# Causal masks of an attention kernel: added in VectorE's maximum instead of by mask products on TensorE

## The reference

```
o1 = _attn(q, k1, v1, causal)          # all keys up to the query's own
o2 = _attn(q, ks, vs)                  # 128 selected keys, no mask
winmask = causal & (ii[:, None] - ii[None, :] < WINDOW)      # WINDOW = 128
o3 = _attn(q, kw, vw, winmask)
o = g[:, 0] * o1 + g[:, 1] * o2 + g[:, 2] * o3
...
s = jnp.einsum('bhqd,bhkd->bhqk', q, k) / np.sqrt(HD)
s = jnp.where(mask, s, -1e9); softmax(s, -1) @ v
```

## Time and profile before

| | |
|---|---|
| median of 3 runs | 2175.93 us (2175.18 to 2177.6) |
| the profiled execution | 2175.96 us |
| its span, first to last instruction | 2174.2 us |
| mean granted TensorE clock | 0.956 of full |
| TensorE busy | 1933.2 us, 89% |
| VectorE, ScalarE, GpSimd busy | 1296.0, 1332.8, 1019.8 us |
| share of TensorE in the chain that ended last | 85% |

### The profile page before, as it was taken

One profiled execution on the slowest core, in us unless ns is written; L12 is line 12 of the kernel. 1 busy time (PEld: TensorE's weight loads), 2 busy tenths in 40 slices (PEclk: granted clock), 3 DMA queues, 4 the chain that ended last, 5 costly groups with the idle time before them and its releaser, 6 DMA issues.

```text
span 2174.2 us, 56981 instructions
## 1 busy us (share of the span) xinstructions
PE 1933.2 (89%) x19452; PEld 1579.1 (73%) x19452; DVE 1296.0 (60%) x3336; ACT 1332.8 (61%) x3520; POOL 1019.8 (47%) x1680
## 2 busy tenths in 40 slices
PE   1123899999999999999999999999999999999769
PEld 0011688878887888788878888888888887888522
DVE  4417466656665666566666666666656665666443
ACT  0022477767776777677766776677767776777232
POOL 6743355535553555445544555455445544554000
PEclk9956799999999999999999999999999999999579
DMA  4100000000000000000000000000000000000000
GB/s 80 25 12 14 12 0 0 2 12 0 0 0 13 0 0 0 13 0 0 0 13 0 0 0 13 0 0 0 13 0 0 0 2 1 0 0 0 1 5 14
DMA packets 21980, 13.51 MB, mean 6 GB/s; under 512 B 17401, under 2 KB 18425, under 8 KB 21953
## 3 DMA queue, kind: packets, MB, share of 16 engines
q1 hardware_dynamic: 18880, 10.03, 1.8%
q0 software_dynamic: 3072, 3.15, 0.8%
HBM read 6.34 MB, written 1.05 MB: 3 GB/s over the span
## 4 chain that ended last, share of the span: by engine, by line
PE 85%; issue 6%; DVE 5%; another core or an unknown queue 2%; ACT 2%; ACTq 0%; DMA 0%; POOLq 0%; DVEq 0%; POOL 0%
PE PT L1082 13%; PE S L1070 13%; PE O L1097 9%; PE S L1073 9%; PE X L1006 7%; PE S L1072 6%; PE X L1014 5%; PE S L1145 3%; PE X L1030 3%; PE X L1023 3%; PE S L1074 2%; PE O L1273 1%; PE O L1192 1%; PE S L1253 1%
## 5 line engine op out<-in xcount | busy, mean ns | idle before, releaser
L464 ACT ACTIVATE big<-S,negm 128x128 f32<-128x128 f32 (+3 forms) x1536 | 576.1, 455 | 49.8 <-DVE negm L765 49.7
L475 ACT ACTIVATE big<-PT 128x384 f16<-128x384 f32 (+3 forms) x1024 | 405.4, 448 | 313.7 <-PE PT L1082 311.9
L773 DVE SCALAR_TENSOR_TENSOR big<-PT,big 128x384 f16<-128x384 f32 (+3 forms) x1024 | 477.1, 503 | 177.7 <-ACT big L475 177.6
L763 DVE TENSOR_REDUCE negm<-S 128x1 f32<-128x128 f32 (+3 forms) x512 | 251.6, 491 | 378.8 <-PE S L1074 377.7
L1082 PE MATMUL PT<-cst,big 128*128 128x128 f32 x2688 | 379.7, 274 | 6.6 <-DVE big L773 6.6
L1070 PE MATMUL S<-k1T,qT 128*128 128x128 f32 (+3 forms) x1024 | 368.8, 442 | 0.6 <-ACT big L464 0.3
L1082 PEld LDWEIGHTS PT<-cst,big 128*128 128x128 f32 x2688 | 303.9, 141 | 41.9 <-issue 5.9
L363 POOL TENSOR_TENSOR osum<-big 128x128 f32<-128x128 f32 x128 | 61.7, 482 | 535.9 <-DVE big L786 535.9
L1097 PEld LDWEIGHTS O<-vh,big 128*128 128x128 f16 x8064 | 277.6, 96 | 15.1 <-issue 8.0
L1097 PE MATMUL O<-vh,big 128*128 128x33 f16 x8064 | 282.3, 178 | 1.4 <-DVE big L773 1.4
L1073 PE MATMUL S<-kwT,qT 128*128 128x256 f32 (+1 forms) x1024 | 278.9, 354 | 0.0
(11 more groups left out here) (252 smaller groups left out, 3012.5 us busy)
## 6 DMA issues: line engine op xcount, KB each, us to landing
lat_b<-lat_all SPq DMA_DIRECT2D x8, 448.0 KB, 2.8
xn_b<-xn_all SPq DMA_DIRECT2D x8, 128.0 KB, 2.5
xnT_b<-xnT_all SPq DMA_DIRECT2D x8, 128.0 KB, 2.3
out_dram<-h_all SPq DMA_DIRECT2D x8, 128.0 KB, 2.0
cst<-in_c_cst_dram SPq DMA_DIRECT2D x1, 608.0 KB, 5.1
big<-in_L_tok_token_emb_dram,idx POOLq DMA_INDIRECT x32
big<-in_L_tok_instr_emb_dram,idx POOLq DMA_INDIRECT x32
big<-in_L_tok_arg_emb_dram,idx POOLq DMA_INDIRECT x32
```

Of the source, the lines that this page charges most:

```text
L464: last = nc.scalar.activation(pr[par][:, lo:lo + n], S[par][:, lo:lo + n], ACT.Exp, bias=negm[par][:, k:k + 1])
L475: nc.scalar.activation(pT[par][:, 0, lo:lo + n], PT[:, lo:lo + n], ACT.Copy, scale=PSCALE).then_inc(s["pT_hi"], 1)
L763: v.tensor_reduce(negm[par][:, 0:1], S[par][:, 0:n1], op=ALU.max, axis=AX.X, negate=True)
L773: last = v.scalar_tensor_tensor(pT[par][:, 1, lo:lo + n], PT[:, lo:lo + n], PSCALE, pT[par][:, 0, lo:lo + n], ALU.mult, ALU.subtract)
```

## The change

The two mask products go, and with them the bf16 identity and the bf16 mask. VectorE's three reductions per tile become three instructions that add a mask from SBUF to the scores, multiply by -1, write the result back over the scores in PSUM, and give the minimum of what they wrote, which is minus the masked maximum. The masks are the constants in fp32: mask_w is the window's, mask_c is 384 columns of zeros and then the causal mask, so that its last n1 columns fit the causal block; the selected keys get zeros. probs reads the negated scores with scale -1. An instruction that does nothing (nop) carries VectorE's wait.

```diff
--- before.py
+++ after.py
@@ -54,8 +54,8 @@
         sin5 = cst[:, K_SIN:K_SIN + 5 * ROPE].rearrange("p (t r) -> p t r", t=5)
         iota_row = cst[:, K_IOTA:K_IOTA + P]
         tri = cst[:, K_TRI:K_TRI + NE * NE].rearrange("p (a b) -> p a b", a=NE)
-        identb = sb("identb", [P, P], bf16)
-        maskb = sb("maskb", [P, 2 * P], bf16)
+        mask_w = cst[:, K_MASK:K_MASK + 2 * P]
+        mask_c = sb("mask_c", [P, T])
         ones = sb("ones", [P, P])
         gamma_b = sb("gamma_b", [P, C])
         beta_b = sb("beta_b", [P, C])
@@ -462,7 +462,7 @@
                 act.wait_ge(s["pT_psum"], U + 1)
                 for k, (lo, n) in enumerate(((0, n1), (4 * P, n2), (5 * P, n3))):
                     last = nc.scalar.activation(pr[par][:, lo:lo + n], S[par][:, lo:lo + n], ACT.Exp,
-                                                bias=negm[par][:, k:k + 1])
+                                                bias=negm[par][:, k:k + 1], scale=-1.0)
                 last.then_inc(s["probs_ready"], 1)
 
             def take_hi(u, t, U):
@@ -627,8 +627,8 @@
 
 
             dve.wait_ge(s["ld_cst"], 16)
-            v.tensor_copy(identb[:], ident)
-            L(v.tensor_copy(maskb[:], cst[:, K_MASK:K_MASK + 2 * P]))
+            v.memset(mask_c[:, 0:T - P], 0.0)
+            L(v.tensor_copy(mask_c[:, T - P:T], cst[:, K_MASK + P:K_MASK + 2 * P]))
             dve.wait_ge(s["ld_w"], 16 * N_W)
             sm = float(HD) ** -0.5
             L(v.tensor_scalar(qw_col[:], qw_col[:], sm, None, ALU.mult))
@@ -760,9 +760,13 @@
                 par = u % 2
                 n1, n2, n3 = kblocks(t)
                 dve.wait_ge(s["scores_ready"], U + 1)
-                v.tensor_reduce(negm[par][:, 0:1], S[par][:, 0:n1], op=ALU.max, axis=AX.X, negate=True)
-                v.tensor_reduce(negm[par][:, 1:2], S[par][:, 4 * P:4 * P + n2], op=ALU.max, axis=AX.X, negate=True)
-                v.tensor_reduce(negm[par][:, 2:3], S[par][:, 5 * P:5 * P + n3], op=ALU.max, axis=AX.X, negate=True).then_inc(s["max_ready"], 1)
+                dve.nop(nofuse=True)
+                for k, (lo, n, m) in enumerate(((0, n1, mask_c[:, T - n1:T]), (4 * P, n2, mask_c[:, 0:n2]),
+                                                (5 * P, n3, mask_w[:, 2 * P - n3:2 * P]))):
+                    z = S[par][:, lo:lo + n]
+                    last = v.tensor_tensor_reduce(out=z, in0=z, in1=m, scale=-1.0, scalar=3.0e38, op0=ALU.add, op1=ALU.min,
+                                                  accum_out=negm[par][:, k:k + 1])
+                last.then_inc(s["max_ready"], 1)
 
             def take_lo(u, t, U):
 
@@ -1068,10 +1072,8 @@
                 n1, n2, n3 = kblocks(t)
                 q = qT[par][:, t * P:(t + 1) * P]
                 mm(z[:, 0:n1], q, k1T[:, 0:n1], start=True, stop=True)
-                mm(z[:, n1 - P:n1], identb[:], maskb[:, P:2 * P], start=False, stop=True, skip_group_check=True)
                 mm(z[:, 4 * P:5 * P], q, ksT[par][:], start=True, stop=True)
-                mm(z[:, 5 * P:5 * P + n3], q, kwT[par][:, (t + 1) * P - n3:(t + 1) * P], start=True, stop=True)
-                mm(z[:, 5 * P:5 * P + n3], identb[:], maskb[:, 2 * P - n3:2 * P], start=False, stop=True, skip_group_check=True).then_inc(s["scores_ready"], 1)
+                mm(z[:, 5 * P:5 * P + n3], q, kwT[par][:, (t + 1) * P - n3:(t + 1) * P], start=True, stop=True).then_inc(s["scores_ready"], 1)
 
             def turn_probs(u, t, U):
                 pe.wait_ge(s["probs_ready"], U + 3)
```

## The result

The changed kernel takes 2122.07 us (median of 4 runs, 2120.38 to 2122.96); the kernel before, run on the same chip beside it, 2175.55 (4 runs, 2174.22 to 2177.6). The ratio is 0.9753, with a 95% interval of 0.9738 to 0.9769. Forecast were 2116 and a range of 2092 to 2180: the sign and the mechanism came out, and the time is 6 us above the point.

The account below looks back on a forecast made before the run. TensorE was taken as the bound, with the path over VectorE and ScalarE to line 1030 exactly as long in a second head. 2176 - 57 (56 trips) - 3 (passages) = 2116 us, range 2092 to 2180.

Parts of the forecast that it names:

- What the masks' removal gives on TensorE: Eight mask products per head and the gaps behind them go: 0.87 us per head, 1.74 per trip of two heads.
- D: The time by which VectorE's set of instructions for one score tile grows; taken as 0.27 us.
- The small part: VectorE's second, small instruction that reads the accumulator after each main part; taken as 0.09 us.
- Where D lands: At line 1030's weight load, behind VectorE and ScalarE; a trip of two heads gains 1.56 - 2D, 1.02 us.
- The passages: A batch's last two heads and the passage to the next: of 1.7 us of masks 0.4 kept per batch, 3 us.
- A: Slower: VectorE's new instruction runs at half rate, set growth 1.09 us for tile 2, together 2248 us; chance 0.14.
- B: VectorE's accumulator read is not overlapped, set growth 0.69 us, 2166 us in all; chance 0.17.
- C: On TensorE the masks' gap of 0.06 us moves to the next weight load, 2136 us in all; chance 0.14.
- No second place: TensorE's wait for take_lo at line 1082 has 0.66 us to spare, so VectorE's growth isn't paid twice while small.

Follow-up runs that it names:

- e2: The changed kernel with the bf16 masks and both mask products put back on TensorE, and VectorE's new instructions adding zeros: 2199.62 us.
- e1: The kernel before without its two mask products and with nothing in their place, VectorE keeping its plain reductions: 2090.68 us.
- e12: The kernel before with the transpose for ksT moved between the first and second branch of tile 3's values: 2157.90 us.
- e10: The changed kernel with the transpose for ksT moved between the first and second branch of tile 3's values: 2071.09 us.
- e8: The kernel before with only a nop added between VectorE's wait and its first reduction: 2183.91 us.
- e5: The changed kernel with the transpose of ksT and ScalarE's copy moved forward to the previous head, ahead of tile 3's values: 2090.85 us.
- e6: The kernel before with the same move of ksT's transpose and copy as in e5: 2160.45 us.
- e11: e10 with the selected keys' block taken first by the plain reduction, which carries VectorE's wait, and without the nop: 2062.57 us.

## Why the prediction was right, and where it was off

- **What bounds the kernel**: right. The path from tile 2's scores over VectorE and ScalarE to line 1030 (now 1034) was as long as TensorE's own work in a second head and had 0.28 to spare in a first. e2 shows both numbers: +0.29 and +0.00.
- **What the masks' removal gives on TensorE**: 1.74 us per trip was forecast from the earlier trace rows. With the wait of 0.23 taken off, 1.51 should be left at D = 0; e1 measured 1.43. On the order without the wait 1.57 remain of 1.74 (e12 to e10). So this term was too high, by 0.08 per trip on the old order and 0.17 on the new. The gap behind the mask did go (0.28 to 0.22); tile 3's causal product took 0.09 back on the new order, the rest is not located.
- **D**: 0.27 was forecast, 0.28 to 0.29 measured (rows of the change, e2). The size is right, the working is not. The small part was priced at 0.09 three times; inside the set it is 0.17 for all three. So main parts of 128 columns start 0.25 apart, not 0.29, and the set ends 1.26 behind its start (1003.14 - 1001.88), not 1.36. The nop was costed at nothing, with the words that it would be part of D if it delayed the start: it does, by 0.07 (e8), and some 0.04 more stand ahead of the set. Two errors have met, and that their sum is D is luck.
- **Where D lands**: a second head 0.23 + D, a first D - 0.05. Measured from e1 to the change: 0.29 and 0.15, so 0.44 per trip where 0.49 was forecast. That and the 0.08 nearly cancel, by luck too: a trip gains 0.99, forecast 1.02. The idle times of the load, forecast at 0.5 and 0.2 and measured at 0.74 and 0.33, were mis-stated: before, the load idled 0.23 in a second head without any loss, and a new wait comes on top of that.
- **The passages**: this is the mis-sized term. "I keep 0.4 per batch, 3 us in all" gave nothing. The stretch of a batch's last two heads and what lies behind them takes 41.26 us in the change and took 41.33 before (686.42 - 645.16, and 700.46 - 659.13, at the load of line 1040 or 1036). Without masks and without D (e1) it takes 40.49. So the masks are worth 0.84 there, and VectorE's growth takes 0.77 back. The timeline of the change shows at which waits:

```profile
647.32 0.42 PEld L1034 LDWEIGHTS X<-cst,kk 128*128 128x128 f32 x4 [0.62 <-ACT ksT L413]
...
662.10 0.64 PEld L1084 LDWEIGHTS PT<-cst,big 128*128 128x128 f32 x6 [0.79 <-DVE big L777]
...
681.05 3.65 PEld L1194 LDWEIGHTS O<-wproj,oT 128*128 128x128 f32 x32 [0.90 <-ACT oT L413]
```

  The same three loads idle 0.36, 0.57 and 0.62 in e1: 0.26, 0.22 and 0.28 less, which makes the 0.77 within rounding. The third idled 0.38 in the earlier trace rows. I had seen it and yet priced only what it covers now, not that D lengthens it. The second is take_lo's, which the prediction weighed inside the heads only.
- **The sum**: the batch period fell from 222.93 to 215.97, eight times 6.96 = 56 us, where 57 + 3 were forecast. The profiled executions differ by 54.6. So of the 6 us missed, nearly 3 are the passages and nearly 2 the trips (0.99 for 1.02, 56 times); the last one or two lie outside the eight batches or within the scatter of the runs.
- **The rivals**: A (half rate) is refuted by 566 ns at 384 columns, where over 0.7 us was its mark. B (no overlap) is refuted by main parts of 128 columns 0.25 apart, where its mark was 0.43. The Trainium skill (VectorE: DVE Perf Modes, The DRAIN you can't avoid), by which B was weighed, has a sentence that I had left out: a next operation that is not held back starts earlier. The trace agrees with that sentence, for the accumulator read too: it starts at 1002.36, and its main part's row ends at 1002.45. C is refuted by line 1075's 0.22: its price was 0.48 per trip, and 0.08 to 0.17 were missing.
- **No second place**: right inside the heads, as the 0.66 to spare there had it. All of line 1084's waits for take_lo (5.5 us of its products, 6.9 of its loads) stand at the passages, in a batch's last two heads, and there take_lo is a second place: the 0.79 above was 0.57 before the change.

## What to carry to other kernels

When work is taken off the busiest engine, look for the wait that already ends level with it, however few microseconds it shows: both the saving beyond it and every cost laid onto its path are lost there. Here 19 us of such waits in the list became 72 in the same row, and the path took over a third of the change's value; moving one transpose by a few instructions gave it back. Test the parts apart and together, since spare time that covers a cost alone may be used up by the gain: e1 and e2 add to -62 us, the change gave -53.5. And when the transpose is moved, check who holds the buffer at the new place (e5 against e10).

## What the runs showed of the hardware

- An instruction on VectorE that adds a second input, writes 384 columns back over its own input in PSUM and accumulates takes 566 ns, the reduction of the same columns 558. At 128 columns it is 325 against 281.
- An accumulator read has a row of 141 ns, but with its main part it delays the next instruction by about 0.05 us only (0.25 against 0.20 from start to start; 0.06 on average in a set of three).
- A nop that carries a wait on VectorE delays what follows by 0.07 us each time, even on an engine that idles 0.7 us ahead of it (e8).
- The place of one transpose of 128 columns per head changed the kernel before by 16 to 18 us (e6, e12), though the list has no wait for another engine in its first heads. The transpose takes 0.32 in a first head, behind the values and a gap of 0.15, 0.16 in a second head, 0.11 behind other transposes (e6) and 0.15 among the values (e12). But with tile 3's causal product it takes 2.27 us per trip at the old place and in e6 alike (0.32 + 0.93 + 0.16 + 0.86, and 0.11 + 0.95 + 0.11 + 1.10): what goes is mainly the gap.
- TensorE's granted clock falls behind the attention in every kernel here, but in e10 it stays at 0.50 through the last projection, and in e11 it is up again (0.98) for 3.4 us of it: 7.07 against 4.93 us for the same work.
